# Third layer norm's weight and bias as rows on VectorE instead of folded into the first MLP matrix

## The reference

```python
def layernorm(x, w, b):
    mu = jnp.mean(x, axis=-1, keepdims=True)
    var = jnp.mean((x - mu) ** 2, axis=-1, keepdims=True)
    return (x - mu) * jax.lax.rsqrt(var + EPS) * w + b
...
x = x + (o @ Wproj + bproj)
h = jax.nn.gelu(layernorm(x, ln3_w, ln3_b) @ W1 + b1, approximate=False)
x = x + (h @ W2 + b2)
```

## Time and profile before

| | us |
|---|---|
| median of 3 runs (406.52 to 407.26) | 406.68 |
| the profiled execution, its own time | 405.8 |
| its span in the profile | 403.9 |
| PE busy | 356.9 |
| DVE busy | 284.6 |
| ACT busy | 238.8 |
| POOL busy | 198.5 |

### The profile page before, as it was taken

How to read it: one execution, slowest core, us unless ns; L and a number is a source line. 1 busy time by engine, 2 the same in 40 slices (tenths; PEclk the granted TensorE clock), 3 DMA queues, 4 the chain that set the end, 5 groups by cost and what they waited for, 6 DMA issues and landing times.

```text
span 403.9 us, 11390 instructions
## 1 busy us (share of the span) xinstructions
PE 356.9 (88%) x4432; PEld 321.8 (80%) x4432; DVE 284.6 (70%) x640; ACT 238.8 (59%) x462; POOL 198.5 (49%) x177
## 2 busy tenths in 40 slices
PE   0678999999999998779999999989889898998984
PEld 0568888888888887669999999989778787887863
DVE  4785398898988967116555445555899999999853
ACT  1242357767677663383466545553788787887762
POOL 2453245344454538100433320508789989899820
PEclk9995799999999999899999999998999999999999
DMA  6943000110000000000000000000000010110001
GB/s 164 232 138 114 24 25 26 27 41 30 26 2 2 23 2 2 2 0 2 2 0 0 0 0 2 7 14 11 10 21 13 26 46 23 45 36 13 28 28 41
DMA packets 15256, 12.58 MB, mean 31 GB/s; under 512 B 3568, under 2 KB 14576, under 8 KB 15216
## 3 DMA queue, kind: packets, MB, share of 16 engines
q1 hardware_dynamic: 14144, 10.91, 9.3%
q10 hardware_dynamic: 1072, 1.11, 1.1%
HBM read 9.92 MB, written 2.10 MB: 30 GB/s over the span
## 4 chain that ended last, share of the span: by engine, by line
PE 57%; issue 22%; DVE 8%; POOL 6%; ACT 4%; DMA 2%; ACTq 0%; POOLq 0%; DVEq 0%
PE bank_qk L668 9%; PE banks_s L716 6%; PE bank_y L798 4%; PE bank_qk L693 4%; PE bank_qk L697 3%; PE banks_s L968 3%; PE bank_t L764 3%; PE bank_y L792 3%; PE bank_o L707 3%; PE bank_t L668 2%; DMA ln_rows<-in_L_xattn_ln_b 2%; PE bank_y L988 2%; DVE row_max L1137 2%; PE bank_y L660 2%; POOL x_all L358 2%
## 5 line engine op out<-in xcount | busy, mean ns | idle before, releaser
L394 POOL TENSOR_TENSOR norm_inv<-norm_sq_min,minus_half 128x32 f32<-128x32 f32 x16 | 87.4, 5466 | 1.8 <-DVE norm_sq_min L1301 1.8
L334 POOL TENSOR_TENSOR masked<-qkT_r,halves_t 128x512 fp32r<-128x512 f32 x32 | 32.8, 1047 | 39.6 <-DVE qkT_r L1127 39.6
L537 ACT ACTIVATE W_s<-banks_s,b_all 128x256 f32<-128x256 f32 x60 | 25.0, 468 | 39.3 <-PE banks_s L847 39.3
L1137 DVE TENSOR_REDUCE row_max<-banks_s 128x8 f32<-128x1024 f32 x32 | 37.6, 1218 | 9.3 <-PE banks_s L716 9.1
L461 ACT ACTIVATE PT<-banks_s 128x1024 f32<-128x1024 f32 x32 | 31.0, 1021 | 21.4 <-PE banks_s L747 21.4
L351 POOL TENSOR_TENSOR b_var_eps<-b_mean_var,eps_t 128x2 f32<-128x2 f32 x8 | 1.6, 197 | 73.1 <-DVE b_mean_var L1075 73.1
L847 PE MATMUL banks_s<-lnT_hi,W_hi 128*128 128x256 f32 x120 | 34.3, 286 | 0.0
L847 PE MATMUL banks_s<-lnT_lo,W_hi 128*128 128x256 f32 x120 | 33.9, 283 | 0.0
L847 PE MATMUL banks_s<-lnT_hi,W_lo 128*128 128x256 f32 x120 | 33.9, 283 | 0.0
L716 PE MATMUL banks_s<-masked,qkT_r 32*128 32x256 f32 x768 | 32.2, 298 | 1.8 <-DVE row_max L1137 1.5
L603 ACT ACTIVATE PT<-banks_s 128x1024 f32<-128x1024 f32 x32 | 31.1, 1025 | 4.1 <-PE banks_s L968 4.1
(11 more groups left out here) (154 smaller groups left out, 1097.5 us busy)
## 6 DMA issues: line engine op xcount, KB each, us to landing
ctx_in<-in_ctx SPq DMA_DIRECT2D x32, 96.0 KB, 2.0
x_all<-in_x SPq DMA_DIRECT2D x16, 128.0 KB, 2.1
W_s<-in_L_xattn_W SPq DMA_DIRECT2D x2, 1024.0 KB, 7.0
out<-Wq_s SPq DMA_DIRECT2D x16, 128.0 KB, 1.7
Wq_s<-in_L_xattn_Wq ACTq DMA_DIRECT2D x1, 256.0 KB, 6.9
Wkv_s<-in_L_xattn_Wkv ACTq DMA_DIRECT2D x1, 256.0 KB, 7.5
Wproj_s<-in_L_xattn_Wproj SPq DMA_DIRECT2D x1, 256.0 KB, 2.9
wout_s<-in_L_xattn_wout SPq DMA_DIRECT2D x1, 256.0 KB, 3.1
```

Source lines behind the costliest of these rows:

```text
L334: nc.gpsimd.tensor_tensor(masked[:, r, 1, :, half, :], qkT_r[:, r, 1, :, :].bitcast(fp32), ones, ALU.mult)\
L394: nc.gpsimd.tensor_tensor(norm_inv[:, j, :], norm_sq_min[:, j, :], minus_half[:, :], ALU.pow)\
L537: last = nc.scalar.activation(hT[:, m, :], bank_s[u][:, 256 * k:256 * k + 256], ACT.Gelu, bias=b1_all[:, m:m + 1])
L1137: v.tensor_reduce(row_max[:, 8 * h:8 * h + 8], banks_s[:, 2 * h:2 * h + 2, :].rearrange("p n (r k) -> p (n r) k", k=TOK), AX.X, ALU.max).t ...
```

## The change

The weight and the bias of the third norm are loaded as rows, the same 256 numbers on each of the 128 partitions, into memory that is otherwise `rot_sq` of the last stage (`ln3_rows`). `normalise_b` becomes four instructions for a pair of tiles instead of two: (x - mean) * weight for both tiles, and, after the wait for rstd, * rstd + bias for both. `mlp_bias`, the addition to b1 and the wait `w_mlp_ready` go; Gelu's bias is b1 itself. `w1_split` has no factor any more: a copy and a difference. The load of `norm_w` keeps its column form in a tensor of its own.

```diff
-        ln_cols = sb("ln_cols", 128, 3, KT)
+        norm_cols = sb("norm_cols", 128, KT)
+        ln3_rows = rot_sq[:, :].rearrange("p (n c) -> p n c", n=2)
...
-            for n, w in enumerate((ln3_w, ln3_b, norm_w)):
-                sp.dma_start(ln_cols[:, n, :], w.rearrange("(t p) -> p t", p=128), allow_slow_non_contiguous=True).then_inc(w_b1_loaded, LOADED)
+            for n, w in enumerate((ln3_w, ln3_b)):
+                sp.dma_start(ln3_rows[:, n, :], w.unsqueeze(0).broadcast_to([128, C1])).then_inc(w_b1_loaded, LOADED)
+            sp.dma_start(norm_cols[:, :], norm_w.rearrange("(t p) -> p t", p=128), allow_slow_non_contiguous=True).then_inc(w_b1_loaded, LOADED)
...
-                    last = nc.scalar.activation(hT[:, m, :], hT[:, m, :], ACT.Gelu, bias=b1_all[:, m:m + 1])
+                    last = nc.scalar.activation(hT[:, m, :], hT[:, m, :], ACT.Gelu, bias=b1_cols[:, m:m + 1])
...
-            act.wait_ge(w_mlp_ready, 1)
+            act.wait_ge(w_b1_loaded, 4 * LOADED)
...
-            mlp_bias()
             step_a(4)
-            pe.wait_ge(w_mlp_ready, 1)
...
                 if u == 0:
                     dve.wait_ge(w1_loaded, LOADED)
-                    dve.wait_ge(w_b1_loaded, 4 * LOADED)
-                scale = ln_cols[:, 0, u % 2:u % 2 + 1]
-                v.tensor_scalar(w1_part(W1_hi, u), w1_part(W1_s, u), scale, None, ALU.mult).then_inc(w1_hi_done, 1)
+                v.tensor_copy(w1_part(W1_hi, u), w1_part(W1_s, u)).then_inc(w1_hi_done, 1)
                 dve.wait_ge(w1_hi_done, u + 1)
-                v.scalar_tensor_tensor(w1_part(W1_lo, u), w1_part(W1_s, u), scale, w1_part(W1_hi, u).bitcast(fp32),
-                                       ALU.mult, ALU.subtract).then_inc(w1_lo_done, 1)
+                v.tensor_tensor(w1_part(W1_lo, u), w1_part(W1_s, u), w1_part(W1_hi, u).bitcast(fp32), ALU.subtract)\
+                    .then_inc(w1_lo_done, 1)
...
                 dve.wait_ge(b_stats, 2 * p + 2)
-                dve.wait_ge(b_rstd, p + 1)
                 if later:
                     dve.wait_ge(b_T, p)
                 for j in range(2):
-                    v.tensor_scalar(b_xn[:, j, :], tile_of(2 * p + j), b_mean_var[:, j, 0:1], b_rstd_t[:, j:j + 1],
-                                    ALU.subtract, ALU.mult).then_inc(b_norm, 1)
+                    v.scalar_tensor_tensor(b_xn[:, j, :], tile_of(2 * p + j), b_mean_var[:, j, 0:1], ln3_rows[:, 0, :],
+                                           ALU.subtract, ALU.mult).then_inc(b_centred, 1)
+                dve.wait_ge(b_rstd, p + 1)
+                for j in range(2):
+                    dve.wait_ge(b_centred, 2 * p + j + 1)
+                    v.scalar_tensor_tensor(b_xn[:, j, :], b_xn[:, j, :], b_rstd_t[:, j:j + 1], ln3_rows[:, 1, :],
+                                           ALU.mult, ALU.add).then_inc(b_norm, 1)
...
-            dve.wait_ge(b1_mm, 1)
-            v.tensor_tensor(b1_all[:, :], bank_y[:, 0:HM], b1_cols[:, :], ALU.add).then_inc(w_mlp_ready, 1)
...
                 elif s == 14:
+                    dve.wait_ge(w_b1_loaded, 4 * LOADED)
                     normalise_b(0, False)
```

More of the change, by code:

```diff
@@ L150, in build @@
         onT_r = sb("onT_r", 128, 2, KT, TOK, dtype=fp32r)
-        ln_cols = sb("ln_cols", 128, 3, KT)
+        norm_cols = sb("norm_cols", 128, KT)
+        ln3_rows = rot_sq[:, :].rearrange("p (n c) -> p n c", n=2)
         b1_cols = sb("b1_cols", 128, HM)
-        b1_all = sb("b1_all", 128, HM)
         bproj_row = sb("bproj_row", 128, C1)
@@ L187, in build @@
         a_padded, w_padded, c_padded = sem("a_padded"), sem("w_padded"), sem("c_padded")
-        ln_rows_loaded, picks_ready, b1_mm, w_mlp_ready = sem("ln_rows"), sem("picks_ready"), sem("b1_mm"), sem("w_mlp_ready")
+        ln_rows_loaded, picks_ready = sem("ln_rows"), sem("picks_ready")
         w1_hi_done, w1_lo_done, w2_hi_done, w2_lo_done = (sem(k) for k in ("w1_hi_done", "w1_lo_done", "w2_hi_done", "w2_lo_done"))
@@ L206, in build @@
             sem(f"c_{k}") for k in ("rope", "turned", "rot", "rot_sq", "norm_sq", "norm_min", "norm_inv", "unit", "unit_hi", "unit_lo"))
-        b_stats_raw, b_stats, b_var, b_rstd, b_norm, b_bias, b_T, b_lnT_hi, b_lnT_lo, b_w1, b_gelu, b_hT_hi, b_hT_lo, b_w2, b_x, b_raw = (
+        b_stats_raw, b_stats, b_var, b_rstd, b_norm, b_bias, b_T, b_lnT_hi, b_lnT_lo, b_w1, b_gelu, b_hT_hi, b_hT_lo, b_w2, b_x, b_raw, b_centred = (
             sem(f"b_{k}") for k in ("stats_raw", "stats", "var", "rstd", "norm", "bias", "T", "lnT_hi", "lnT_lo", "w1", "gelu",
-                                    "hT_hi", "hT_lo", "w2", "x", "raw"))
+                                    "hT_hi", "hT_lo", "w2", "x", "raw", "centred"))
         block = es.enter_context(nc.Block())
@@ L537, in gelu_b @@
                         last = nc.scalar.activation(hT[:, m, :], bank_s[u][:, 256 * k:256 * k + 256], ACT.Gelu,
-                                                    bias=b1_all[:, m:m + 1])
+                                                    bias=b1_cols[:, m:m + 1])
                     last.then_inc(b_gelu, 1)
@@ L653, in _ @@
             mm = nc.tensor.matmul
-            def mlp_bias():
-                pe.wait_ge(w1_loaded, LOADED)
-                pe.wait_ge(w_b1_loaded, 4 * LOADED)
-                for m in range(HM):
-                    for k in range(KT):
-                        last = mm(bank_y[:, m:m + 1], W1_s[:, k, 128 * m:128 * m + 128], ln_cols[:, 1, k:k + 1],
-                                  start=k == 0, stop=k == KT - 1)
-                last.then_inc(b1_mm, 1)
             def split_mm(out, a, b):
@@ L1247, in _ @@
             for k in range(KT):
-                scale = ln_cols[:, 2, k:k + 1]
+                scale = norm_cols[:, k:k + 1]
                 hi, lo, w = by_tile(wq_r[:, 0, k, :]), by_tile(wq_r[:, 1, k, :]), by_quad(wq_s[:, k, :])
```

## The result

The changed kernel takes **400.68 us** (median of 4 runs, 400.54 to 401.64) against 406.66 us for the kernel before beside it (4 runs, 406.52 to 407.26). The ratio is 0.9855, with a 95% interval of 0.9837 to 0.9873. The same kernel, run once more later, took 401.76 us (median of 4 runs, 400.63 to 402.76), ratio 0.9872 (0.9845 to 0.9898); its median had been expected to stay at 400.7. Over all eight runs it is 401.2.

What follows compares the result with a forecast made beforehand. PE, busy for 88% of the span, was taken as the bound, with 6.85 us of small products on the path. -6.85 - 0.32 + 0.2 + 0.4 = -6.57 us took 406.68 to 400.1 us; range 396.9 to 402.1.

Steps and rivals of the forecast that it cites:

- The small products: Pipeline fill, stage A: removing the 32 products of W1 with the bias column saves 6.85 us, no stall replacing them.
- The start of the queries at 34.8: Fill: tile 3's queries start at 34.8 to 34.9 us, right behind the shifted scores, instead of 41.65.
- The return of the clock at 38.7: Fill: 2.4 GHz returns at about 38.7 us, as long after full-width work starts as before; then the sum stands.
- the first rival: Clock returns earlier in the fill (1.2 to 1.8 us) and stage A's tail dip may vanish (1.7); 396.6 to 399.3, 28%.
- The split of W1: DVE's two splits without a factor take 2.12 instead of 2.44 us; 0.32 us less, all of it counted.
- The loads: Two column loads become two of 128 KB, behind W1 and ahead of tile 4 in SP's queue; 0 us taken.
- Step 14: Pair 0's norm on DVE takes 0.95 us more; with 0.8 slack, PE loses 0.2 us.
- POOL held up by the subtractions: Rival at pairs 2 and 7: POOL's rstd instructions wait for both new subtractions; +1.6 us, 401.7 us, 10%.
- Pairs 2 and 7: Stage B, where PE waits for the norm: each loses 0.2 us before the turning, 0.4 us together.
- the second rival: DVE's two-input subtractions hold up POOL's rstd at pairs 2 and 7, 1.0 instead of 0.2 each; +1.6 us, 10%.
- The tail: End of stage A: pair 1's norm costs 0; the first rival had its slow stretch perhaps vanishing, worth 1.7 us.
- Pairs 3 to 6: Stage B: slack of 2.07 us absorbs the 0.2 us; low halves wait for ACT anyway; 0, pairs stay at 11.95.

Runs made afterwards that it cites:

- late addition: Changed kernel with POOL's two additions of the second MLP bias, from pair 2 on, held until DVE has made the low halves; 400.05 us, ratio 0.9834.
- the kernel before with the late addition: Kernel before, with POOL's additions of the second MLP bias held back until DVE's four low-half subtractions are through; 407.24 us, ratio 1.0017.
- warm tail: Six unread products in PE's waits before the weighted values of tiles 14 and 15: 399.12 us on the changed kernel, 398.36 us with POOL's additions also held back.

## Why the prediction was right, and where it was not

Forecast 400.1 us, range 396.9 to 402.1; measured 400.68, and 401.76 in the second set of runs. The main term holds; one term, at pairs 2 and 7, was mis-sized by 1.6 us. By its steps:

- **The small products: right.** -6.85 forecast; the kernel without them is 6.9 and 6.6 us shorter than the two traces of before, so hardly any wait took their place. The half-rate price under it was seen too: 3.60 us at the full clock.
- **The start of the queries at 34.8: wrong in this trace, by the clock.** They start at 36.39, as the keys and values of tile 1 ran at the low level, which the trace of before does not have. In the trace with the late addition they start at 34.5, and the kernel before with the late addition has a low stretch at 20 to 24 us too, so it is no cost of the change. Nor is it a loss that can be counted on: in both traces of after it is there, in the trace of the late addition and of the one with a warm tail added to it, it is not.
- **The return of the clock at 38.7: not right.** It came at 37.6, 1.2 us after the queries began and not 3.9. That is the first rival, which I priced at up to 1.8 us. It brought 1.3, and the late start took 1.6, so both canceled to within 0.3 us. That the fill gained 6.89 us, close to the sum, in this pair of traces is luck: in the trace with the late addition the clock came back 3.2 us after the queries began, no stretch was low at tile 1, and the turning of `on` stands 7.8 us ahead of before.
- **The split of W1: right.** 45.72 - 43.59 = 2.13 us for two splits against 2.44, and PE's wait behind it fell from 0.64 to 0.33.
- **The loads: right.** 0 forecast; PE has no wait in front of the queries of tile 4.
- **Step 14: right.** 0.27 lost (6.89 to 6.62), 0.2 forecast. Both new lines take 0.48 us:

```profile
L1069 DVE SCALAR_TENSOR_TENSOR qk_unit<-x_all,b_mean_var,rot_sq x16: 472/478/520, 127.3 to 249.8; 128x256 f32<-128x256 f32 x16
```
```profile
L1074 DVE SCALAR_TENSOR_TENSOR qk_unit<-qk_unit,b_rstd_t,rot_sq x16: 476/480/487, 128.1 to 250.8; 128x256 f32<-128x256 f32 x16
```

- **POOL held up by the subtractions: did not happen** at the place named. DVE waits 0.20 us for rstd, and PE's wait at pair 2 is 0.68.
- **Pairs 2 and 7: the term that failed.** 0.2 each was forecast, by PE's wait before the turning, and that part came (0.19 and 0.14). The step that failed is its silence on what follows: "the low halves behind it wait for ACT anyway: 0", written of pairs 3 to 6 and tacitly extended. At pairs 2 and 7 they wait for nobody, they run back to back beside POOL's additions, and PE needs them soon. They became 1.08 us longer, which cost PE 0.86 and 0.79. The two pairs cost 2.0 us in all instead of 0.4. It is the exclusion of DVE and POOL that the second rival priced at +1.6 us for these same pairs, only at other instructions. The trace of before had the sign of it: POOL's additions at 3.50 us for two at pair 2, where those of the loop took 2.16:

```profile
205.28 2.16 POOL L358 TENSOR_TENSOR x_all<-x_all,b_row 128x256 f32 x2 [0.97 <-DVE qk_unit L1083]
```

- **The tail: two low stretches for one,** 1.3 us lost, against the hope of the first rival that the dip might vanish. The second trace of before has two as well.
- **Pairs 3 to 6: right,** 11.95 us and no wait of PE; even twice the subtractions leave them there.

For the profiled executions the account closes. The measured terms -6.85 - 0.31 + 0.27 + 1.98 give -4.91 us, and the spans differ by 4.9; what the clock did (-1.6 and +1.3 in the fill, -1.3 in the tail, +1.5 in stage C) cancels. The forecast for this execution was 397.3 us of span and 399.2 of time, measured 399.0 and 400.76: 1.6 to 1.7 too low, all of it pairs 2 and 7. The median was missed by 0.6 only, because the forecast put it 0.9 above the profiled execution, as it was before, and in the four runs of after the two were equal. That is luck as well; against the second set of runs the forecast is 1.7 too low.

## What to carry to other kernels

- Where an engine's work grows beside another's, look at what comes next on both, not only at the grown part: an order of two engines that happened to suit the one on the path can flip. Holding the harmless one back with a wait on the other took the choice away (1.36 us in the traces for one line; the medians show 0.6 and 1.7).
- The many tiny products on TensorE cost twice here: their own time, and the clock behind them. Where waits of one to two microseconds could not be closed, unread products in them kept the clock up and made the time repeat; that was worth 6.8 us by the medians on top of the change with the held-back addition (400.05 to 393.27), and 5.5 by the spans, about as much as the change itself.
- A gain read from one trace with a falling clock has an error of 1 to 2 us from the clock alone. A second trace of the same kernel shows it at little cost.

## What the hardware showed that I had not expected

- One-column products, back to back for 3.6 us at 2.4 GHz (3.73 us busy, 32 of them), were followed, 0.5 us behind their end, by the low level from 38 to about 41.4 us. In the trace of the changed kernel, which has no such products, the clock stayed.
- DVE's four two-input subtractions of 128x512 and POOL's two additions of 128x256 take 2.49 and 3.50 us in some kernels, 3.57 and 2.14 in others, with the same start to 0.01 us. Each kernel keeps its way: before and after did in both of their traces, and after also with a warm tail.
- The moments at which the clock falls and rises shift against the work between two executions of one kernel; the tail of stage A of the kernel before had one low stretch in one trace and two in another. With the idle time filled, four of six runs agreed to 0.2 us.
